# Second layer's edges: target scores loaded, turned and carried half by half; table rows with masked scores

## The reference, cut to what matters

```python
for r in range(R):                                   # R = 4 relations, H = 4 heads of D = 32
    mask = (edge_type == r)[:, None]
    h = (x @ W[r]).reshape(N, H, D)
    e_src = jnp.einsum('ehd,hd->eh', h[src], attn_src[r])
    e_dst = jnp.einsum('ehd,hd->eh', h[dst], attn_dst[r])
    e = jax.nn.leaky_relu(e_src + e_dst, negative_slope=0.2)
    e_for_max = jnp.where(mask, e, -1e+30)
    e_max = jnp.maximum(jax.ops.segment_max(e_for_max, dst, num_segments=N), 0.0)
    e_exp = jnp.where(mask, jnp.exp(e - e_max[dst]), 0.0)
    e_sum = jax.ops.segment_sum(e_exp, dst, num_segments=N)
    alpha = e_exp / (e_sum[dst] + 1e-08)
    msg = alpha[:, :, None] * h[src]
    out = out + segment_sum(msg, dst).reshape(N, H * D)
```

## Time and profile before

| | value |
|---|---|
| median of 3 runs | 4801.82 us |
| span of the profiled execution | 4790.3 us |
| what lies around that span, against the median | 11.5 us |
| DVE / POOL / ACT / PE busy, whole program | 74% / 70% / 57% / 43% |
| stage of the change | 1495.8 to about 2593 us of the span |

### The profile page before, as it was taken

How to read it: one execution, slowest core, us unless ns; L and a number is a source line. 1 busy time by engine, 2 the same in 40 slices (tenths; PEclk the granted TensorE clock), 3 DMA queues, 4 the chain that set the end, 5 groups by cost and what they waited for, 6 DMA issues and landing times. The chain is left out here.

```text
span 4790.3 us, 58561 instructions
## 1 busy us (share of the span) xinstructions
PE 2063.5 (43%) x11050; PEld 1159.6 (24%) x11189; DVE 3526.3 (74%) x6949; ACT 2744.0 (57%) x6085; POOL 3345.1 (70%) x2986
## 2 busy tenths in 40 slices
PE   0778999999863000000000400000000259989985
PEld 0434444444422000000000200000000135555553
DVE  5545555555536899999997578888888667777776
ACT  0667778888722888888885323223222246666663
POOL 4578888888726777777772477777777337777775
PEclk8899999999976555555555755555555679999998
DMA  8965555555633577777775456666666323433332
GB/s 310 295 173 99 95 95 101 102 101 101 130 71 130 204 258 273 254 279 261 269 262 199 139 186 214 214 218 217 211 211 217 117 57 118 129 119 122 123 118 84
DMA packets 287089, 823.57 MB, mean 172 GB/s; under 512 B 63541, under 2 KB 178885, under 8 KB 276994
## 3 DMA queue, kind: packets, MB, share of 16 engines
q1 hardware_dynamic: 105564, 562.09, 31.2%
q0 software_dynamic: 172176, 255.22, 24.4%
q10 hardware_dynamic: 9238, 5.24, 0.4%
HBM read 371.98 MB, written 450.34 MB: 172 GB/s over the span
## 5 line engine op out<-in xcount | busy, mean ns | idle before, releaser
L661 POOL DMA_INDIRECT tab<-arena x560 | 942.3, 1683 | 239.7 <-issue 133.2
L801 PE MATMUL psum<-arena 128*128 128x512 bf16 (+1 forms) x4592 | 929.7, 357 | 7.3 <-issue 1.7
L1604 PE MATMUL psum<-ident,arena 128*128 128x128 f32 x15 | 3.7, 426 | 2150.1 <-DVEq L1632 2150.1
L1976 POOL DMA_INDIRECT arena<-table,arena x784 | 749.2, 956 | 242.1 <-issue 238.5
L2476 POOL DMA_INDIRECT arena<-table,arena x622 | 616.2, 991 | 193.9 <-issue 181.3
L1359 POOL DMA_INDIRECT arena<-table,arena x588 | 613.2, 1043 | 179.3 <-issue 170.5
L2558 PE MATMUL psum<-arena 128*128 (+2 forms) x4023 | 674.7, 330 | 84.1 <-DVE arena L2600 41.4
L801 PEld LDWEIGHTS psum<-arena 128*128 128x128 bf16 x4704 | 435.0, 99 | 477.8 <-issue 31.9
L1604 PEld LDWEIGHTS psum<-ident,arena 128*128 128x128 f32 x15 | 2.7, 212 | 2150.7 <-DVEq L1632 2150.4
L2558 PEld LDWEIGHTS psum<-arena 128*128 (+1 forms) x4050 | 400.9, 99 | 354.6 <-issue 102.3
L1407 ACT ACTIVATE arena<-arena 128x128 f32<-128x128 f32 x1344 | 409.1, 387 | 94.4 <-DVE arena L1526 90.7
(11 more groups left out here) (425 smaller groups left out, 5101.3 us busy)
## 6 DMA issues: line engine op xcount, KB each, us to landing
rows<-arena SPq DMA_DIRECT2D x56, 3808.0 KB
arena<-seg_rows SPq DMA_DIRECT2D x112, 896.0 KB, 7.1
rows<-arena SPq DMA_DIRECT2D x56, 1008.0 KB, 4.7
rows<-arena SPq DMA_DIRECT2D x56, 896.0 KB
seg_rows<-arena SPq DMA_DIRECT2D x36, 896.0 KB
arena<-table,arena POOLq DMA_INDIRECT x1994
arena<-src_lanes SPq DMA_DIRECT2D x56, 448.0 KB
seg_rows<-arena SPq DMA_DIRECT2D x10, 1792.0 KB
```

The lines of the kernel that those rows point to most:

```text
L661: eng.indirect_dma_start(out=m.tabs[j], out_offset=bass.IndirectOffsetOnAxis(ap=idx[g][:, k:k + 1], axis=0), in_=rows[g][:, k, 0:D], in_of ...
L801: t = eng.matmul(ps[:, c, 0:w], part[n // 2 % PAIRS][:, n % 2, :], hot[n % HOTS][:, lo:lo + w], start=False, stop=False, skip_group_check= ...
L1976: eng.indirect_dma_start(out=kv[k][:, j, :], out_offset=None, in_=m.table2, in_offset=bass.IndirectOffsetOnAxis(ap=idx[k][:, j:j + 1], axi ...
```

## The change

The target scores are no longer prepared for the whole stage. SP loads the 16 scores of 14 columns (`ed_in`, one load for each half, four in flight); ACT copies them from column-major to score-major order into `ed[k % 2]` and puts the last column of the half before in front (`turn_scores`, two activations); and DVE carries them with a scan of 240 words, which is the new `score` step 0. The table rows hold 16 score words instead of 4: those of the row's own relation, and minus 1e30 in the other twelve. So `HS` goes from 132 to 144 words, step 1 adds 16 by 14 words, which are masked already, and step 2 is the leaky ReLU over 16 by 14. The masks `all_keeps` get four buffers, as they are needed three halves ahead (`AHEAD1`).

```diff
-HS = D + H1
+HS = D + RH
@@ layer0_nodes
+                for t in tab:
+                    v.put(eng.memset(t[:, :, D:HS], -BIG))
-                        eng.tensor_copy(tab[b % TAB_TILES][:, :, D:HS], sc[:, 0:RH].rearrange("p (r h) -> p r h", h=H1)).then_inc(tab_e, 1)
+                        eng.tensor_copy(own_scores[b % TAB_TILES], sc[:, 0:RH].rearrange("p (r h) -> p r h", h=H1)).then_inc(tab_e, 1)
@@ layer1_edges, SP
-                for c in range(PARTS):
-                    t0, t1 = c * T // PARTS, (c + 1) * T // PARTS
-                    eng.dma_start(ed_all[:, t0:t1, :], lanes(m.seg_dst)[:, t0:t1, :]).then_inc(ed_in[c], 16)
+                def load(i, k):
+                    eng.dma_start(ed_in[k % RING], lanes(m.seg_dst)[:, edges(i, k), :]).then_inc(ed_landed[k % RING], 16)
+                        hold(eng, ed_turned, 2 * nth(i, k) + 2)
+                        if not last:
+                            load(i, k + RING)
                         hold(eng, summed, sums_before(i, k) + SUMS1)
                         hold(eng, filled, 2 * nth(i, k) + 4)
                         eng.dma_start(lanes(m.rows1)[:, edges(i, k), :], rows[k % 2]).then_inc(stored, 16)
@@ layer1_edges, ACT
+                def turn_scores(i, k, before):
+                    hold(eng, ed_landed[k], 16 * i + 16)
+                    eng.activation(ed[k % 2][:, :, 1:COLS], ed_in[k].rearrange("p t a -> p a t"), ACT.Copy).then_inc(ed_turned, 1)
+                    eng.activation(ed[k % 2][:, :, 0], before, ACT.Copy).then_inc(ed_turned, 1)
...
                         hold(eng, summed, sums_before(i, k))
+                        if k + AHEAD1 < RING or not last:
+                            spread_keeps(*half(i, k + AHEAD1))
+                            hold(eng, scored, SCORES1 * nth(i, k + AHEAD1 - 1) + 2)
+                            turn_scores(*half(i, k + AHEAD1), ed[(k + AHEAD1 - 1) % 2][:, :, HALF])
                         stage_keeps(*half(i, k + 1))
                         eng.wait_ge(rows_free, nth(i, k) + 1)
                         fill((k - 1) % RING)
@@ layer1_edges, DVE
-                for c in range(PARTS):
...
-                        eng.tensor_tensor_scan(ed_all[:, t0:t1, k], m.keep[:, t0:t1], ed_all[:, t0:t1, k], before, ALU.mult, ALU.add).then_inc(ed_steps, 1)
...
-                eng.tensor_tensor(ed4, ed4, spread(m.other_rel[:, :, :], 3, [P, T, REL, H1]), ALU.add).then_inc(ed_steps, 1)
-                eng.tensor_tensor(two, two, ed_all[:, :, 2 * H1:RH], ALU.max).then_inc(ed_steps, 1)
-                f.then(eng.tensor_tensor(ed, ed_all[:, :, 0:H1], ed_all[:, :, H1:2 * H1], ALU.max))
...
                     if step == 0:
+                        eng.wait_ge(ed_turned, 2 * nth(i, k) + 2)
+                        eng.wait_ge(all_kept, nth(i, k) + 1)
+                        ed_cols = ed[k % 2].rearrange("p a t -> p (a t)")
+                        ins = eng.tensor_tensor_scan(ed_cols, all_keeps[k], ed_cols, 0.0, ALU.mult, ALU.add)
+                    elif step == 1:
                         eng.wait_ge(landed[k], 16 * HALF * (i + 1))
                         eng.wait_ge(marks, nth(i, k) + 1)
-                        ins = eng.tensor_tensor(score4, feat[k][:, :, D:HS], ed[:, edges(i, k), :], ALU.add)
-                    elif step == 1:
-                        ins = eng.scalar_tensor_tensor(out=score4, in0=score4, scalar=0.2, in1=score4, op0=ALU.mult, op1=ALU.max)
+                        ins = eng.tensor_tensor(now, feat[k][:, :, D:HS].rearrange("p t a -> p a t"), ed[k % 2][:, :, 1:COLS], ALU.add)
                     elif step == 2:
-                        ins = eng.tensor_tensor(now.rearrange("p (r a) t -> p t r a", a=H1), spread(score4, 2, [P, HALF, REL, H1]),
-                                                spread(m.other_rel[:, edges(i, k), :], 3, [P, HALF, REL, H1]), ALU.add)
+                        ins = eng.scalar_tensor_tensor(out=now, in0=now, scalar=0.2, in1=now, op0=ALU.mult, op1=ALU.max)
```

More of the change, by code:

```diff
@@ L939, in layer0_nodes @@
         ed = A(NB, RH)
-        tab = [A(REL, HS) for _ in range(TAB_TILES)]
+        tab_cols = [A(REL * (HS + H1) + D) for _ in range(TAB_TILES)]
+        tab = [t[:, 0:REL * HS].rearrange("p (r f) -> p r f", f=HS) for t in tab_cols]
+        own_scores = [t[:, D:D + REL * (HS + H1)].rearrange("p (r f) -> p r f", f=HS + H1)[:, :, 0:H1] for t in tab_cols]
         ps = m.psum
@@ L1250 @@
 SCORES1 = 3 + 3
+AHEAD1 = 3
 OLD1 = 3
@@ L1269, in layer1_edges @@
         rows = [states[:, h * HALF * R1:(h + 1) * HALF * R1].rearrange("p (t f) -> p t f", f=R1) for h in range(2)]
-        ed_all = states[:, 0:T * RH].rearrange("p (t f) -> p t f", f=RH)
-        ed = A(T, H1)
+        ed_in = [A(HALF, RH) for _ in range(RING)]
+        ed = [A(RH, COLS) for _ in range(2)]
         apart_sb = A(HALF - IN_PSUM, REL * D)
@@ L1277, in layer1_edges @@
         feat.append(m.xT[:, 0:W].rearrange("p (t f) -> p t f", f=HS))
-        e, fwd, *top = ([m.xT[:, W + k * RH * COLS:W + (k + 1) * RH * COLS].rearrange("p (a t) -> p a t", t=COLS) for k in range(5)]
-                        + [A(RH, COLS)])
+        e, fwd, *top = ([m.xT[:, W + k * RH * COLS:W + (k + 1) * RH * COLS].rearrange("p (a t) -> p a t", t=COLS) for k in range(4)]
+                        + [A(RH, COLS) for _ in range(2)])
         gap = [A(RH, COLS) for _ in range(2)]
@@ L1283, in layer1_edges @@
         weight = [m.psum[:, h, RH * COLS:RH * COLS + APART * H1].rearrange("p (t a) -> p t a", a=H1) for h in range(2)]
-        score4 = A(HALF, H1)
         old = m.lane_end[:, 0:REL * D]
         keeps = [A(HALF) for _ in range(2)]
-        all_keeps = [A(RH * COLS) for _ in range(2)]
+        all_keeps = [A(RH * COLS) for _ in range(RING)]
         resets = [A(RH * COLS + 1) for _ in range(2)]
@@ L1292, in layer1_edges @@
         SUM, MAX = REL * D, REL * D + RH
-        PARTS = 4
-        ed_in, ed_first_in = [sem(f"dst_scores_landed{c}") for c in range(PARTS)], sem("first_scores_landed")
-        begun, ed_steps = sem("buffers_begun"), sem("dst_scores_steps")
+        ed_landed, ed_first_in = [sem(f"dst_scores_landed{k}") for k in range(RING)], sem("first_scores_landed")
+        begun, ed_turned = sem("buffers_begun"), sem("dst_scores_turned")
+        all_kept = sem("keeps_spread")
         scored, weighed, summed = sem("score_steps"), sem("weight_steps"), sem("sum_steps")
@@ L1346, in _ @@
                         eng.nop().then_inc(rows_free, 1)
+                for k in range(RING):
+                    load(0, k)
+                with eng.Fori(0, LOOPS - 1) as i:
+                    turn(i, False)
+                turn(LOOPS - 1, True)
             @block.gpsimd
@@ L1382, in _ @@
                 eng.nop().then_inc(direct, DIRECT * RING)
-                eng.wait_ge(begun, 8)
+                eng.wait_ge(begun, 10)
+                for k in range(AHEAD1):
+                    spread_keeps(0, k)
+                eng.wait_ge(ed_first_in, 16)
+                turn_scores(0, 0, ed_first)
                 for k in range(2):
```

31 lines of the change are left out of this document (13 added, 18 removed).

## The result

The changed kernel takes 4817.11 us (median of 19 runs, 4807.41 to 4828.99), the kernel before 4798.93 us (19 runs, 4787.49 to 4812.78): a ratio of 1.0039 [1.0029, 1.0048]. It is slower, by 0.4%; the forecast was 4775, and 4817 lies outside the range.

What follows compares the result with a forecast made beforehand. POOL's gathers were taken to bound the stage, DVE having about 0.95 us to spare a half. POOL's sum gave -26.9 us, the loop's -30.6 + 2.7 = -27.9; taken as -27, from 4801.8 to 4775, range 4750 to 4803.

Steps and rivals of the forecast that it cites:

- the head goes: Stage head: without scans and wide operations the loop starts near 1548.3, 30.6 us earlier; POOL's 26.3 us count.
- DVE in a half: DVE per loop half: 0.98 us removed, 1.43 added, +0.45 (+0.11 to +0.75); own half 17.70 us, paid from waits.
- quick lock: Loop rival, chance 0.18: gathers' lengthening falls from 0.8 to 0.3 us a half; 4761, or 4750 at 17.8 us.
- the row-by-row sum: Loop pace: DVE's half 17.70 us; POOL's lengthening grows 0.05 us a half, 2.7 us over 54, about 18.25 us.
- ACT and the store: Loop: added ACT work fits its idle time; store at T + 5.2 after `add_up` starts, cover shrinks from 4 to 0.6 us.
- Bad lock: Loop rival, chance 0.23: gathers meet DVE's two-input operations more; lengthening 1.1 (mild, 4791) to 1.9 us a half (4834).
- no relief: Head rival, chance 0.05 (with nothing gained otherwise): POOL was never held by DVE's operations, its 1046 us stay; 4802.

Runs made afterwards that it cites:

- the 63: Changed kernel plus 63 empty DVE instructions: in the head 4779.9 us (0.9967); directly ahead of DVE's loop, with ACT's body moved by 64, 4745.76 us (0.9910).
- the three kernels without fetches and in the quick phase: Changed kernel, ACT's body moved by 64, plus 31 empty DVE instructions (0.9929), both bodies moved and `fill` first (0.9917), or 63 directly ahead of DVE's loop (0.9910).
- the kernel before moved to the bad place: Kernel before with 65 empty instructions on DVE ahead of the loop, its body at 834: 4797.58 us against 4788.6, 1.0016.
- the 20 us of the wide operations: Kernel before without the head's three wide DVE operations, a memset in their place: 4767.44 us, 0.9961; last gather ends 20.3 us earlier.

## Why the prediction was wrong, by its steps

**The step that failed is one that is not in it.** The part on the head counted the instructions that go by their time alone. They also went out of DVE's instruction stream ahead of the loop, which put the loop's body at a place where it is fetched anew in each turn: 3.0 + 1.74 us, 12 times, 57 us. In the prediction's terms, *the head goes* took only time away, and *DVE in a half* was to be paid out of DVE's waits; the cost of the jump back stood at nothing in both. The removal of 63 instructions has no row in the trace of before, but the instruction queue stood on its page, and the difference of the two streams was at hand. Expected was that DVE does not wait ahead of its first instruction in `add_up`; it does, 12 times in the changed kernel, and there not for the store.

The Trainium skill (Runtime: NRT & Kernel Launch, Instruction fetch mechanics) says that a taken branch whose target is not among the instructions held makes the engine wait for a fetch. The trace agrees, and adds how much and when: nothing or 4.7 us a turn for the same 285 instructions. The page counts 256 instructions to a block of 16 KiB. By that a packet of 8 KiB is 128 instructions, and the runs show 128 as the length after which the place repeats (706 and 834 both bad, 737 and 769 both good), where the page's block would give 256.

**The head: right.** The first `add_up` was forecast 50.5 us after the first gather (1548.3 - 1497.84), and comes after 50.0. The lengthening of gathers in the head falls from 26.7 to 0.7 us.

**The pace of the loop: the wrong rival was likeliest.** Forecast was 18.25 us with POOL as the bound, with "quick lock" beside it at 0.18. It came out as that rival says, whenever DVE does not stall and the 63 do not stand in the head: the gathers' lengthening falls from 41.1 to 29.1 us over the loop, and DVE with its 17.91 us is the bound. By little: with the 63 ahead of the loop all 784 gathers take 1002.8 us, 3.7 of which wait for ACT, so that POOL needs 17.84 us for 14. The rival's price was -41 us or 4761, at best 4750; the three kernels without fetches and in the quick phase gained 0.71, 0.83 and 0.90%, 34 to 43 us. The argument for it, two engines nearly even so that POOL may run ahead, deserved more than the row-by-row sum that kept POOL the bound by 0.55 us a half. Nothing in the sum could tell which way the phase would move, and both phases occurred in these kernels. The size of the stall's damage hangs on it: with POOL the bound it cost 9 us in the kernel before moved to the bad place, and by that measure the forecast gain of 27 us would have outlived it.

**DVE in a half: +0.45 was too low.** The three added operations, by form (mean ns behind the comma):

```profile
L1492 DVE TENSOR_TENSOR_SCAN arena<-arena 128x240 f32<-128x240 f32 x56 | 36.4, 651 | 1.6 <-ACT arena L1395 1.6
L1496 DVE TENSOR_TENSOR xT<-arena 128x224 f32<-128x224 f32 x42 | 22.1, 526 | 32.1 <-DMA arena<-table,arena 31.5 <-issue 0.6
L1498 DVE SCALAR_TENSOR_TENSOR xT<-xT 128x224 f32<-128x224 f32 x56 | 21.6, 386 | 0.1
```

Together 1.56 us instead of 1.43. The scan (0.65) and the leaky ReLU (0.38) were right; the addition over 224 words with a strided input takes 0.53 and not the 0.40 of the unstrided row, near the upper bound of 0.54. DVE's own half is 17.91 us, forecast 17.70 with bounds of 17.36 and 18.00. From 17.25 that is +0.66; the durations give +0.58, and where the other 0.08 goes is open.

**ACT and the store: right, with less cover than it sounds.** The timeline of SP's store behind the stalled and behind an ordinary start of `add_up`:

```profile
2018.85 0.35 SPq L1353 DMA_DIRECT2D rows<-arena  x1
2036.73 0.35 SPq L1353 DMA_DIRECT2D rows<-arena  x1
```

The latter is T + 5.1 (2036.73 - 2031.62), forecast T + 5.2. SP's wait for a store, against the earlier trace rows:

```profile
SPq L92 <- DMA rows<-arena: 559.8, 47, 12.9
```

11.9 us a store instead of 12.0. Rows were free 3.7 us before `add_up` needed them in the kernel before and are 0.8 us before in the changed one (medians; the forecast was 4 and 0.6). DVE has no wait of over 0.1 us for the store in the changed kernel, and it has one once in most turns of the kernel with 31 empty instructions, where ACT's own fetches make `fill` late. The wider table rows cost the gathers nothing (0.944 us at the median in both).

**Bad lock and no relief.** The first did not happen in the changed kernel, but its mild half did with 63 instructions in the head, some 18.55 us a half. The second is refuted by the head, and by the 20 us of the wide operations.

## What to carry to other kernels

A loop's body has a place in its engine's instruction stream, and an edit ahead of it moves that place: count it, look at the instruction queue's packets per turn and at "issue" waits right behind the jump back, and try a few empty instructions before you judge the edit. An "issue" wait elsewhere can be another thing, as the store here: look up which signal came last. When the edit also moves the bound to the engine that jumps, its stalls, hidden until then, count in full. Where two engines come out nearly even, the loop can run in more than one steady state; here the one in which POOL had run ahead was the more frequent, and the range should hold both.

## What was not expected of the hardware

- Instructions come in pieces of 8192 bytes, 128 instructions. A loop body on DVE of 285 or 286 costs no fetch or five a turn by its place within 128: none beginning at 737 or 769, five at 706 or 834. ACT's, of 312 and 333, costs five beginning at 426 and 437, none 64 further on. All this fits bodies that lie in three pieces being kept and such in four not, if some 34 to 61 instructions stand ahead of those that the build counts; that offset was not seen.
- On DVE the jump back so costs 3.0 us at once (1.6 to 2.1 in the kernel before moved to the bad place) and 1.7 a few instructions later; on ACT single waits of 2.9 and 3.2 us.
- An addition over 224 words with a strided input takes 0.53 us on DVE, a leaky ReLU over as many without a stride 0.39.
- The same 63 instructions in front of a loop of 1000 us and not in the head, which starts it 2 us later, went with a pace of 17.91 instead of 18.55 us a half (0.9910 and 0.9994 of the kernel before).
